# A fused MoE, MoE, attention and FFN kernel: set-up reordered, the second half's routing rescheduled, attention maxima held in 16-bit halves

## The chip, the cores and the metric

The kernel runs on one core of one Trainium2 chip as a single program. The metric is the device time of one execution in microseconds. The engines are TensorE (PE, whose weight loads PEld overlap its matmuls), VectorE (DVE), ScalarE (ACT), GpSimd (POOL) and the queues that start DMA transfers (SP, and those of ACT, DVE and POOL).

## The reference, cut to what matters

x is 32 x 128 x 128, so 4096 tokens of width 128; ctx has the same shape. Four residual layers follow one another, each on a layer norm of x:

```python
x = x + moe_a(layernorm(x), ctx)    # 8 experts 128->512->128, relu; router on ctx, top 2, softmax of the two
x = x + moe_b(layernorm(x))         # 16 experts 128->128->128, silu(x W1+b1)*(x W3+b3); sigmoid scores,
                                    # best 2 of 4 groups, top 4 of 16, weights * 2.5 / their sum
x = x + attention(layernorm(x), ctx, ctx)  # 16 heads of 8, masked to earlier keys, softmax(q k / sqrt(8)) v
x = x + 0.5 * ffn(layernorm(x))     # integer weights scaled, 128->512->128 with silu

def attention(q, k, v):             # qh, kh, vh: heads of 8 columns
    mask = triu(ones(S, S), k=0); mask[0, 0] = False
    scores = where(mask, -inf, qh @ kh.T * scale)
    return softmax(scores) @ vh @ Wo.T + bo
```

The softmax needs the maximum of each row of scores, which is subtracted before the exponential.

## The kernel before

Tokens lie on partitions in tiles of 128; four tiles make a block of 512 (NT = 4), and there are 8 blocks (NB), in two halves of 4 (BH). The tensor X holds the running x for all blocks. fp32 products are built of a rounded high and a low half (`..h`, `..l`), so a weight is first copied by `split_high` (ACT) and `split_low` (DVE, POOL).

**Set-up.** The context's logits choose two experts for each token. Each expert's first weight is "folded" (one row is subtracted from the others): TensorE's `fold(k)`, L1809 to L1813, then on ACT a copy out of PSUM (L1499) and `split_high(k)` (L1471). TensorE's `prefix` (L1789 to L1794) counts tokens per expert and tile into cb_ps, which DVE's `tile_bases` (L836) reads; `inverse` turns slots into token numbers, which DVE casts to idx_sa (L899, `inverted`). ACT's `table_a` writes the normalised tokens of the first half to memory (a_tokens: L1485, L1492). POOL's `gather_slots` (L639) then gathers tokens by expert.

**Stage A** has 39 steps for each half, **stage B** 35 (SB) for each half. A step is one tile of 128 x 4 tokens of one expert (A) or of a group of four experts (B): TensorE transposes the gathered rows when a tile group begins (L1836), multiplies up and down, ACT applies the function, DVE forms products and the low halves (L1241 and L1244, L1252). The rows of results go to memory and are gathered back per token by POOL (`gather_a`, L647; `gather_b`, L669), and DVE adds them to X (`combine_a`, L1013 to L1021).

**The routing of the next stage** is done in the background: `background(h, T)` is called on DVE (L1137), ACT (L1545) and TensorE (L1885) at the end of step T of a half, and does what the tables of L273 to L279 put there. Each table has an entry per half: h = 0 (the first four blocks) runs in stage A's second half, h = 1 in stage B's first. CMB is `combine_a`, STT the statistics, APP the normalised rows, FWD the transposes, LOG the logits, SGM the sigmoid, GRP and MSK the choice of groups, PRE the counts, TOP the best four, POS the slots' bases, WTS the weights, HOT, EID and INV the inversion, SLT the cast of the slots to idx_sb, which POOL waits for before the second half's gathers. Nothing schedules at run time: each engine's instructions stand in program order, and semaphores join them. POOL's queue order is written out by hand (`gather_slots`, `gather_a`, `gather_b` and powers).

**Stage C** is the attention: 32 steps `tau`, each a block and one of four groups of four heads. TensorE computes the scores twice, by rows (`scores`, L2070 and L2071) for the maxima, and transposed (`scores_T`, L2082) for the exponentials; POOL masks the exponentials (L761, `mask_keys`); L2094 multiplies by the values. DVE takes the negated maxima (L1302, `max_of`) into negmax, and `split_max` writes them as two halves (a bf16 high part and the rest) into two columns of nmpad, a part of the tile brows. TensorE transposes nmpad (L2121) into tr_ps, and DVE adds the result to the queries (L1319), so that the next product subtracts the maximum. **Stage D** is the FFN.

## Time and profile before

| | |
|---|---|
| median of 3 runs | 1053.17 us (1051.47 to 1054.09) |
| profiled execution | 1050.84 us |
| its span | 1049.0 us |
| PE, PEld busy | 811.3 (77%), 621.0 (59%) |
| DVE, ACT, POOL busy | 636.2 (61%), 500.6 (48%), 395.2 (38%) |
| mean granted clock of TensorE | 0.876 |

By stretch, from the windows of the trace (us; busy us):

| stretch | us | PE | DVE | ACT | POOL | clock |
|---|---|---|---|---|---|---|
| set-up, 0 to 44.6 | 44.60 | 26.10 | 31.66 | 21.04 | 20.24 | 0.78 |
| stage A, to 370 | 325.40 | 238.54 | 160.49 | 132.35 | 106.67 | 0.85 |
| stage B, to 734 | 364.00 | 262.21 | 195.18 | 168.97 | 132.00 | 0.83 |
| stage C, to 982 | 248.00 | 224.87 | 198.28 | 127.51 | 134.02 | 0.98 |
| stage D, to 1049 | 67.00 | 59.57 | 50.56 | 50.77 | 2.29 | 0.93 |

An engine's busy time against the length of its stretch says how near that stage is to the engine's limit; the chain of waits says which engine's work or signal came last at each moment. "Another core or an unknown queue" in it is a semaphore event whose sender the profile does not name. "Issue" is time in which an engine waited for nothing that the profile shows. A row "x4" is four instructions one after another, whose time runs from the first start to the last end; matmuls overlap, so the time that a group of them really takes is read from the start of the group to the start of the next row.

### The profile page before, as it was taken

The page shows a single profiled execution, that of the slowest core. Times are in us where ns is not written, and L with a number is a line of the kernel's source. Part 1 is how long each engine was busy: PE and PEld are TensorE (multiplying, and loading weights), DVE is VectorE, ACT ScalarE, POOL GpSimd, SP SyncE. Part 2 cuts the span into 40 slices and gives each one's busy share as a digit, 9 for nine tenths or more (in the row PEclk, how much of TensorE's full clock was granted, in tenths as well). Part 3 has the DMA queues.
Part 4 walks back from the last instruction along what each step waited for, and adds up shares of the span by engine and source line. Part 5 has one row for each costly group of instructions (what it writes and reads, how often), then busy time and mean ns, then how long its engine had stood idle before and what let it go on. Part 6 is the DMA issues. An engine that isn't in the chain of part 4 may idle for free.

```text
span 1049.0 us, 17575 instructions
## 1 busy us (share of the span) xinstructions
PE 811.3 (77%) x5374; PEld 621.0 (59%) x5374; DVE 636.2 (61%) x1897; ACT 500.6 (48%) x984; POOL 395.2 (38%) x462
## 2 busy tenths in 40 slices
PE   6577187885789843769877566799789999989898
PEld 4475176764678733657666455688455555555575
DVE  5766053443555812557695344586778888887596
ACT  4443043442465422347644234476255555546586
POOL 5435733005510073443104545410466644446200
PEclk9589678898898965978988868799899999999899
DMA  8482246454311221171021131110344544543011
GB/s 286 132 269 92 87 116 196 164 200 145 103 49 39 71 67 27 42 282 41 23 66 44 53 102 42 57 29 22 105 129 133 139 119 118 165 114 107 5 31 50
DMA packets 96368, 106.54 MB, mean 102 GB/s; under 512 B 12604, under 2 KB 70348, under 8 KB 94999
## 3 DMA queue, kind: packets, MB, share of 16 engines
q1 hardware_dynamic: 76856, 78.04, 23.8%
q0 software_dynamic: 8608, 18.22, 6.8%
q10 hardware_dynamic: 10816, 9.16, 2.8%
q8 instruction: 48, 0.79, 0.3%
q14 instruction: 40, 0.33, 0.1%
HBM read 69.19 MB, written 36.18 MB: 100 GB/s over the span
## 4 chain that ended last, share of the span: by engine, by line
PE 50%; another core or an unknown queue 13%; issue 12%; DVE 11%; ACT 7%; POOL 3%; ACTq 1%; DMA 1%; SPq 1%; DVEq 0%; POOLq 0%
PE y_ps L1872 4%; PE y_ps L2094 3%; PE y_ps L1999 3%; PE hid_ps L1984 3%; PE hid_ps L1860 2%; PE hid_ps L2070 2%; PE hid_ps L2071 2%; PE hid_ps L2082 2%; PE hid_ps L1968 2%; PE tr_ps L2149 2%; PE hid_ps L1850 2%; PE tr_ps L2121 1%; PE hid_ps L1852 1%; PE hid_ps L1969 1%
## 5 line engine op out<-in xcount | busy, mean ns | idle before, releaser
L639 POOL DMA_INDIRECT xr<-b_tokens,idx_sb x70 | 67.0, 957 | 152.6 <-DVE idx_sb L899 105.7
L1121 DVE TENSOR_TENSOR hl<-hid_ps,hh 128x512 fp32r<-128x512 f32 x78 | 53.8, 690 | 110.7 <-ACT hh L1530 73.6
L1872 PE MATMUL y_ps<-region,hh 128*128 x312 | 91.8, 371 | 27.9 <-DVE hl L1121 16.6
L647 POOL DMA_INDIRECT yg<-a_rows,idx_a x64 | 60.9, 952 | 91.8 <-DMA a_rows<-yo 63.3
L1302 DVE TENSOR_REDUCE negmax<-hid_ps 128x4 f32<-128x512 f32 x128 | 85.8, 684 | 8.9 <-PE hid_ps L2071 7.9
L1872 PEld LDWEIGHTS y_ps<-region,hh 128*128 128x128 f32 x312 | 64.8, 208 | 37.0 <-issue 36.6
L1984 PE MATMUL hid_ps<-ident,zb 128*128 128x128 f32 x280 | 49.5, 306 | 45.9 <-DVE hl L1252 24.2
L1860 PE MATMUL hid_ps<-ident,zb 128*128 128x128 f32 x312 | 53.7, 301 | 38.8 <-issue 24.3
L1524 ACT ACTIVATE zb<-hid_ps 128x512 f32<-128x512 f32 x78 | 46.6, 597 | 77.1 <-PE hid_ps L1852 38.8
L1999 PE MATMUL y_ps<-region,hh 128*128 x280 | 82.1, 369 | 0.1
L1241 DVE TENSOR_TENSOR zb<-hid_ps,sg 128x256 f32<-128x256 f32 x70 | 29.7, 424 | 85.5 <-ACT sg L1626 51.3
L2071 PE MATMUL hid_ps<-region 128*128 128x512 f32 x128 | 76.5, 599 | 0.0
L669 POOL DMA_INDIRECT yg<-b_rows,idx_b x64 | 61.3, 958 | 38.6 <-issue 36.7
L1984 PEld LDWEIGHTS hid_ps<-ident,zb 128*128 128x128 f32 x280 | 38.2, 158 | 63.4 <-issue 39.0
L1860 PEld LDWEIGHTS hid_ps<-ident,zb 128*128 128x128 f32 x312 | 43.6, 157 | 53.6 <-issue 27.7
L1620 ACT ACTIVATE sg<-hid_ps 128x512 f32<-128x512 f32 x70 | 41.7, 596 | 68.4 <-PE hid_ps L1970 34.6
L1874 PE MATMUL y_ps<-region,hl 128*128 x312 | 73.1, 234 | 0.0
L1252 DVE TENSOR_TENSOR hl<-hid_ps,hh 128x512 fp32r<-128x512 f32 x70 | 47.9, 684 | 31.4 <-issue 19.8
L1633 ACT ACTIVATE hh<-hid_ps 128x512 fp32r<-128x512 f32 x70 | 41.0, 585 | 54.4 <-remote 28.4
L1874 PEld LDWEIGHTS y_ps<-region,hl 128*128 128x128 f32 x312 | 65.9, 211 | 0.0
L2001 PE MATMUL y_ps<-region,hl 128*128 x280 | 65.5, 234 | 0.2 <-issue 0.2
L761 POOL TENSOR_SCALAR_AFFINE_SELECT sg<-sg 128x512 f32<-128x512 f32 x64 | 40.6, 634 | 58.9 <-ACT sg L1682 58.9
(354 smaller groups left out, 2365.1 us busy)
## 6 DMA issues: line engine op xcount, KB each, us to landing
region<-k_strips SPq DMA_DIRECT2D x128, 64.0 KB
region<-k_strips SPq DMA_DIRECT2D x32, 256.0 KB
region<-hl SPq DMA_DIRECT2D x128, 64.0 KB
k_strips<-k_halves SPq DMA_DIRECT2D x24, 256.0 KB
region<-nought SPq DMA_DIRECT2D x6, 1024.0 KB
a_rows<-yo SPq DMA_DIRECT2D x20, 256.0 KB
b_rows<-yo SPq DMA_DIRECT2D x18, 256.0 KB
staged<-a_w_in SPq DMA_DIRECT2D x16, 256.0 KB, 5.8
```

Of the source, the lines that this page charges most:

```text
L639: g.indirect_dma_start(xr[:, q % 3, j * RB:j * RB + w], None, src, bass.IndirectOffsetOnAxis(ap=rows.bitcast(U32), axis=0)).then_inc(x_got ...
L647: g.indirect_dma_start(yg[:, b % 2, k, j * P:(j + 1) * P], None, ys[h], bass.IndirectOffsetOnAxis(ap=idx[:, h, k, t:t + 1].bitcast(U32), a ...
L669: g.indirect_dma_start(yg[:, b % 2, k, j * P:(j + 1) * P], None, ys_b[h], bass.IndirectOffsetOnAxis(ap=idx_b[:, h, k, t:t + 1].bitcast(U32 ...
L1121: v.tensor_tensor(hl[:, n % 2, :], hid_ps[2 + n % 2][:], hh[:, n % 2, :].bitcast(F32), ALU.subtract).then_inc(a_hl, 1)
L1302: v.tensor_reduce(negmax[:, s % 2, b, :], hid_ps[b % 2][:].rearrange("p (i k) -> p i k", i=HG), AX, ALU.max, negate=True).then_inc(c_max, 1)
L1860: ins = t.transpose(hid_ps[2 + n % 2][:, cs], zb[:, n % 2, cs], ident[:])
L1872: t.matmul(y[:, c0:c0 + 2 * P], hh[:, n % 2, cs], w2a[:, bass.ds(e * (2 * FA) + c * 2 * P, 2 * P)], start=c == 0, stop=False)
L1874: t.matmul(y[:, c0:c0 + P], hl[:, n % 2, cs], w2a[:, bass.ds(e * (2 * FA) + c * 2 * P, P)], start=False, stop=False)
L1984: ins = t.transpose(hid_ps[3][:, es], zb[:, m % 2, es], ident[:])
L1999: t.matmul(y[:, c0:c0 + 2 * P], hh[:, m % 2, es], w2b[:, bass.ds(g * (2 * BT) + e * 2 * P, 2 * P)], start=e == 0, stop=False)
L2001: ins = t.matmul(y[:, c0:c0 + P], hl[:, m % 2, es], w2b[:, bass.ds(g * (2 * BT) + e * 2 * P, P)], start=False, stop=e == EG - 1)
L2071: t.matmul(hid_ps[b % 2][:], qp[s % QPS][:, b * P:(b + 1) * P], kdiag[s % KDS][:, b, :], start=False, stop=True).then_inc(c_s1, 1)
```

## The change

Three parts.

1. **Tables for the second half (h = 1).** The four combines move from steps 3, 7, 11, 15 to 5, 10, 14, 18, with the statistics in the same step instead of the next; what follows them moves too, down to the cast of the slots, from step 31 to 32. HOT (28) and INV (30) stay.
2. **Set-up.** ACT unfolds weights 0 to 3, writes the four tables of tokens, and then unfolds 4 to 7; before it unfolded all eight first. TensorE's counts (`prefix`) stand between fold 3 and fold 4. ACT's wait for in_last comes after the first copy.
3. **Maxima.** nmpad is a bf16 tile instead of fp32. The tile nm16 and one of the two casts are gone, the subtraction reads the high half from nmpad itself, and TensorE's four fp32 transposes are four bf16 matmuls against a bf16 identity.

```diff
--- before.py
+++ after.py
@@ -161,7 +161,7 @@
         att = wideflat[:, 0:2 * BT].rearrange("p (s v) -> p s v", s=2)
         cpad = brows[:].bitcast(F32)
         osb = cpad[:, 0:BT]
-        nmpad = cpad[:, BT:2 * BT].rearrange("p (b h r) -> p b h r", b=NT, h=HG)
+        nmpad = brows[:, 2 * BT:3 * BT].rearrange("p (b h r) -> p b h r", b=NT, h=HG)
         accT = yo
         scales = yg[:, 0]
         d_mv = rt[:, 0:NB * NT * 2].rearrange("p (b t k) -> p b t k", b=NB, t=NT)
@@ -173,7 +173,6 @@
         v_out, wkv = flat(sg[:])[:, 0:VW], flat(sg[:])[:, VW:VW + 2 * P]
         b2h = sb("b2h", [P, 1])
         negmax = sb("negmax", [P, 2, NT, HG])
-        nm16 = sb("nm16", [P, 2, NT, HG], BF16)
         rden = sb("rden", [P, NT, HG])
         b2b = sb("b2b", [EB, P])
         combT = xnt[0:EB, :]
@@ -270,13 +269,13 @@
             T = n % S
             return T % 2 == 1 or T == S - 1
 
-        CMB = ((6, 9, 13, 18), (3, 7, 11, 15))
...
+        CMB = ((6, 9, 13, 18), (5, 10, 14, 18))
...
         SGM, GRP, MSK, PRE, TOP, POS, WTS, HOT, EID, INV, SLT = (
-            (23, 20), (24, 22), (25, 23), (25, 24), (28, 23), (26, 25), (30, 27), (31, 28), (34, 31), (33, 30), (35, 31))
+            (23, 23), (24, 24), (25, 25), (25, 25), (28, 26), (26, 26), (30, 28), (31, 28), (34, 32), (33, 30), (35, 32))
         CH, PAIRS = 4, 8
         ESC = 2
         KVB = (4, 5, 0, 1, 2, 3, 6, 7)
@@ -1307,9 +1306,8 @@
                 eng.wait_ge(c_max, NT * s + NT)
                 if s:
                     eng.wait_ge(c_nmt, s)
-                link(v.tensor_copy(nm16[:, s % 2], negmax[:, s % 2]))
-                v.tensor_copy(nmpad[:, :, :, 3 * HD], nm16[:, s % 2])
-                v.tensor_tensor(nmpad[:, :, :, 3 * HD + 1], negmax[:, s % 2], nm16[:, s % 2], ALU.subtract).then_inc(c_nm, 1)
+                link(v.tensor_copy(nmpad[:, :, :, 3 * HD], negmax[:, s % 2]))
+                v.tensor_tensor(nmpad[:, :, :, 3 * HD + 1], negmax[:, s % 2], nmpad[:, :, :, 3 * HD], ALU.subtract).then_inc(c_nm, 1)
 
             def shift_queries(s):
 
@@ -1493,19 +1491,25 @@
 
             for b in range(BH):
                 load_x(b)
-            eng.wait_ge(in_last, 16)
-            for k in range(EA):
+            def unfold(k):
                 eng.wait_ge(fold_mm, k + 1)
                 a.activation(fold_buf(k)[0:P - 1, :], hid_ps[k % 4][0:P - 1, :], ACT.Copy).then_inc(folded, 1)
                 eng.wait_ge(folded, k + 1)
+                if k == 0:
+                    eng.wait_ge(in_last, 16)
                 split_high(k)
+
+            for k in range(EA // 2):
+                unfold(k)
             eng.wait_ge(nb_ready, 1)
             table_a(0)
             table_a(1)
             eng.wait_ge(nb_ready, 2)
             table_a(2)
             table_a(3)
-            for k in range(8, NRAW_A):
+            for k in range(EA // 2, EA):
+                unfold(k)
+            for k in range(EA, NRAW_A):
                 split_high(k)
 
             def x_high(q):
@@ -1813,10 +1817,12 @@
                 t.matmul(hid_ps[k % 4][:], less_last, raw_buf(k), start=True, stop=True).then_inc(fold_mm, 1)
 
             logits(0)
-            for k in range(EA):
+            for k in range(EA // 2):
                 fold(k)
             eng.wait_ge(chosen, 1)
             prefix(EA, 0)
+            for k in range(EA // 2, EA):
+                fold(k)
             for c in range(CH):
                 inverse(0, c, GA * NT, flat((xr[:], raw[:])[c // 2]).bitcast(F16), flat(yo[:]).bitcast(F16))
             logits(1)
@@ -2118,7 +2124,8 @@
                         eng.wait_ge(c_norm, tau - 1)
                     last_block_use(tau - 1)
                     for b in range(NT):
-                        ins = t.transpose(tr_ps[:, b * P:(b + 1) * P], nmpad[:, b].rearrange("p h r -> p (h r)"), ident[:])
+                        ins = t.matmul(tr_ps[:, b * P:(b + 1) * P], nmpad[:, b].rearrange("p h r -> p (h r)"), ident16[:],
+                                       start=True, stop=True)
                     ins.then_inc(c_nmt, 1)
                 if 0 <= tau + 3 < STEPS:
                     scores(tau + 3, 1)
```

**Order on ACT in set-up.** staged holds the folded weights (one of four PSUM buffers hid_ps is copied into it), region1 the rounded ones, wide the normalised tokens. Before:

```order
L1471 ACTIVATE region1<-staged 128x512 [waits in_raw0,folded]
L1499 ACTIVATE staged<-hid_ps0 127x512 [waits fold_mm]
L1471 ACTIVATE region1<-staged 128x512 [waits in_raw1,folded]
L1499 ACTIVATE staged<-hid_ps1 127x512 [waits fold_mm]
L1471 ACTIVATE region1<-staged 128x512 [waits in_raw1,folded]
L1499 ACTIVATE staged<-hid_ps2 127x512 [waits fold_mm]
L1471 ACTIVATE region1<-staged 128x512 [waits in_raw1,folded]
L1499 ACTIVATE staged<-hid_ps3 127x512 [waits fold_mm]
L1471 ACTIVATE region1<-staged 128x512 [waits in_raw1,folded]
L1485 ACTIVATE wide<-X,nbias,rstds 128x127 [waits nb_ready]
L1485 ACTIVATE wide<-X,nbias,rstds 128x127 x3
L1492 DMA a_tokens<-wide 128x4x128 [waits row_a]
```

Now:

```order
L1469 ACTIVATE region1<-staged 128x512 [waits in_raw0,folded]
L1483 ACTIVATE wide<-X,nbias,rstds 128x127 [waits nb_ready]
L1483 ACTIVATE wide<-X,nbias,rstds 128x127 x3
L1490 DMA a_tokens<-wide 128x4x128 [waits row_a]
L1483 ACTIVATE wide<-X,nbias,rstds 128x127 x4
L1490 DMA a_tokens<-wide 128x4x128 [waits row_a]
L1483 ACTIVATE wide<-X,nbias,rstds 128x127 [waits nb_ready]
L1483 ACTIVATE wide<-X,nbias,rstds 128x127 x3
L1490 DMA a_tokens<-wide 128x4x128 [waits row_a]
L1483 ACTIVATE wide<-X,nbias,rstds 128x127 x4
L1490 DMA a_tokens<-wide 128x4x128 [waits row_a]
L1496 ACTIVATE staged<-hid_ps0 127x512 [waits fold_mm]
```

Before, all eight folds (hid_ps0 to hid_ps3 twice) stand ahead of the first row of wide; now four do, and the fifth fold's copy out of hid_ps0 comes behind the fourth store to a_tokens.

**Order on DVE at the end of stage B's first half.** small, raw and gsel are small tiles of the routing, idx_b and idx_sb the row numbers that POOL gathers by; zb and hl belong to the step's products, yo to the rows of results, xTl to the transposed tokens of the second half. Before:

```order
L882 TENSOR_TENSOR raw<-raw 128x32 [waits dve]
L883 TENSOR_TENSOR idx_b<-raw 128x32 [waits dve]
L899 CAST idx_sb<-cb_ps 128x36 [waits inv_mm]
L1241 TENSOR_TENSOR zb<-hid_ps2,sg 128x256 [waits b_hT,b_up,b_sw]
L1244 SCALAR_TENSOR_TENSOR zb<-hid_ps2,w4,sg 128x128 x2
L1252 TENSOR_TENSOR hl<-hid_ps3,hh 128x512 [waits b_down,b_hh]
L1129 TENSOR_TENSOR yo<-yo,y_ps1 128x256 [waits b_yc]
L1241 TENSOR_TENSOR zb<-hid_ps1,sg 128x256 [waits b_hT,b_up,b_sw]
L1244 SCALAR_TENSOR_TENSOR zb<-hid_ps1,w4,sg 128x128 x2
L1252 TENSOR_TENSOR hl<-hid_ps3,hh 128x512 [waits b_down,b_hh]
L1105 TENSOR_TENSOR xTl<-tr_ps,xTh 128x512 [waits b_up,s_xh]
```

Now:

```order
L851 CAST eid_b<-small 128x36 [waits dve]
L853 TENSOR_TENSOR gsel<-small,firsts 128x144
L878 TENSOR_SCALAR raw<-raw 128x32
L879 TENSOR_SCALAR raw<-raw 128x32
L880 TENSOR_SCALAR raw<-raw 128x32
L881 TENSOR_TENSOR raw<-raw 128x32 [waits dve]
L882 TENSOR_TENSOR idx_b<-raw 128x32 [waits dve]
L898 CAST idx_sb<-cb_ps 128x36 [waits inv_mm]
L1240 TENSOR_TENSOR zb<-hid_ps1,sg 128x256 [waits b_hT,b_up,b_sw]
L1243 SCALAR_TENSOR_TENSOR zb<-hid_ps1,w4,sg 128x128 x2
L1251 TENSOR_TENSOR hl<-hid_ps3,hh 128x512 [waits b_down,b_hh]
L1104 TENSOR_TENSOR xTl<-tr_ps,xTh 128x512 [waits b_up,s_xh]
```

Before, the cast of idx_sb (with the small operations on raw ahead of it, of which two are shown) stood ahead of two steps' work on zb and hl and of the sum into yo; now one step's zb and hl are left behind it, and then comes the second half's xTl.

**Order on DVE in stage C.** hid_ps are the scores, brows is the tile in which nmpad lies, region1 the queries. Before:

```order
L1302 TENSOR_REDUCE negmax<-hid_ps1 128x4 [waits c_s1]
L1310 CAST nm16<-negmax 128x16 [waits c_nmt,c_max]
L1311 CAST brows<-nm16 128x16 [waits dve]
L1312 TENSOR_TENSOR brows<-negmax,nm16 128x16
L1399 TENSOR_TENSOR region1<-y_ps1,region1 128x512 [waits c_qh]
L1302 TENSOR_REDUCE negmax<-hid_ps0 128x4 [waits c_nm,c_s1]
L1319 TENSOR_TENSOR hl<-region2,tr_ps 128x512 [waits q_ld0,c_nmt]
```

Now:

```order
L1301 TENSOR_REDUCE negmax<-hid_ps1 128x4 [waits c_s1]
L1309 CAST brows<-negmax 128x16 [waits c_nmt,c_max]
L1310 TENSOR_TENSOR brows<-negmax,brows 128x16 [waits dve]
L1397 TENSOR_TENSOR region1<-y_ps1,region1 128x512 [waits c_qh]
L1301 TENSOR_REDUCE negmax<-hid_ps0 128x4 [waits c_nm,c_s1]
L1317 TENSOR_TENSOR hl<-region2,tr_ps 128x512 [waits q_ld0,c_nmt]
```

Two casts and a subtraction became one cast and a subtraction, and the subtraction waits for the cast (dve) where the second cast waited for the first.

## Rows read from the trace of the kernel before

**Rows 1.** The page's part 4: the chain by engine, shares of the span.
```profile
PE 50%; another core or an unknown queue 13%; issue 12%; DVE 11%; ACT 7%; POOL 3%; ACTq 1%; DMA 1%; SPq 1%; DVEq 0%; POOLq 0%
```

**Rows 2.** Stage C by windows: us, busy us per engine (instructions), clock, DMA share, GB/s.
```profile
734.00:982.00 248.00, 224.87 (x1865) 130.10 (x1864) 198.28 (x541) 127.51 (x223) 134.02 (x174) 0.98 0.44 120
```

**Rows 3.** Timeline of ScalarE in set-up: start us, us, instruction, [idle before <-releaser].
```profile
24.84 0.63 ACT L1471 ACTIVATE region<-staged 128x512 fp32r<-128x512 f32 x1
...
25.38 1.63 ACT L1485 ACTIVATE wide<-X,nbias,rstds 128x127 f32<-128x127 f32 x4
...
33.32 0.37 ACTq L1492 DMA_DIRECT2D a_tokens<-wide  x1
```

**Rows 4.** Timeline of set-up on the other engines: same columns.
```profile
21.20 0.15 DVE L970 SCALAR_TENSOR_TENSOR nbias<-mvs,rstds 128x8 f32<-128x8 f32 x1
...
23.63 0.42 DVE L836 SCALAR_TENSOR_TENSOR zb<-cb_ps,firsts 128x256 f32<-128x256 f32 x1 [2.28 <-PE cb_ps L1794]
...
35.61 0.20 DVE L899 CAST idx_sa<-cb_ps 128x40 int32<-128x40 f32 x1
...
37.55 1.15 POOL L639 DMA_INDIRECT xr<-a_tokens,idx_sa  x1 [13.12 <-DMA a_tokens<-wide]
...
44.62 1.11 PE L1836 MATMUL tr_ps<-ident,xr 128*128 128x128 f32 x4 [2.24 <-DMA xr<-a_tokens,idx_sa]
```

**Rows 5.** Timeline of VectorE: a combine of the second half.
```profile
420.64 2.32 DVE L1021 SCALAR_TENSOR_TENSOR X<-yg,gates,X 128x128 f32<-128x128 f32 x8
```

**Rows 6.** The chain of waits in stage B's first half: start us, us, what.
```profile
378.80 10.23 another core or an unknown queue
...
436.63 8.54 another core or an unknown queue
```

**Rows 7.** GpSimd alone by windows: us, busy us (instructions), clock, DMA share, GB/s.
```profile
364.30:404.40 40.10, 30.51 (x32) 0.66 0.24 67
...
557.50:572.40 14.90, 11.41 (x12) 0.77 0.27 72
572.40:580.20 7.80, 0.00 (x0) 1.00 0.13 43
```

**Rows 8.** Timeline round the end of stage B's first half.
```profile
547.65 1.09 PE L1984 MATMUL hid_ps<-ident,zb 128*128 128x128 f32 x4 [2.31 <-DVE hl L1252]
...
555.62 0.60 PE L1984 MATMUL hid_ps<-ident,zb 128*128 128x128 f32 x4
...
557.17 0.19 DVE L899 CAST idx_sb<-cb_ps 128x36 int32<-128x36 f32 x1
...
558.95 0.63 PE L1984 MATMUL hid_ps<-ident,zb 128*128 128x128 f32 x4 [0.42 <-DVE hl L1252]
...
563.98 0.66 PE L1836 MATMUL tr_ps<-ident,xr 128*128 128x128 f32 x4 [3.54 <-DMA xr<-b_tokens,idx_sb]
```

**Rows 9.** Timeline of TensorE: bf16 counts of set-up, and stage C.
```profile
22.49 0.22 PE L1789 MATMUL cb_ps<-m,before 128*128 128x128 bf16 x1
22.54 0.65 PE L1791 MATMUL cb_ps<-m,ones 128*128 128x120 bf16 x15
...
846.82 0.66 PE L2121 MATMUL tr_ps<-ident,brows 128*128 128x128 f32 x4
847.32 0.38 PE L2070 MATMUL hid_ps<-maskq,ident 128*128 128x512 bf16 x1
...
853.95 0.63 PE L2121 MATMUL tr_ps<-ident,brows 128*128 128x128 f32 x4 [0.47 <-DVE region L1375]
```

**Rows 10.** Timeline of stage C; last row: L1311's group, min/median/max ns.
```profile
846.02 0.63 POOL L761 TENSOR_SCALAR_AFFINE_SELECT sg<-sg 128x512 f32<-128x512 f32 x1 [0.80 <-ACT sg L1682]
846.11 0.58 DVE L1311 CAST brows<-nm 128x16 f32<-128x16 bf16 x1
...
846.59 0.17 DVE L1312 TENSOR_TENSOR brows<-negmax,nm 128x16 f32<-128x16 f32 x1
...
L1311 DVE CAST brows<-nm x32: 182/588/626, 737.6 to 961.6; 128x16 f32<-128x16 bf16 x32
```

More of the change, by code:

```diff
@@ L271, in ends_pair @@
             return T % 2 == 1 or T == S - 1
-        CMB = ((6, 9, 13, 18), (3, 7, 11, 15))
-        STT = ((7, 10, 14, 19), (4, 8, 12, 16))
-        APP = ((11, 13, 17, 20), (7, 11, 15, 17))
-        FWD = ((13, 15, 19, 22), (9, 13, 17, 19))
-        LOG = ((14, 16, 20, 23), (10, 14, 18, 20))
+        CMB = ((6, 9, 13, 18), (5, 10, 14, 18))
+        STT = ((7, 10, 14, 19), (5, 10, 14, 18))
+        APP = ((11, 13, 17, 20), (9, 14, 18, 20))
+        FWD = ((13, 15, 19, 22), (11, 16, 20, 22))
+        LOG = ((14, 16, 20, 23), (12, 17, 21, 23))
         SGM, GRP, MSK, PRE, TOP, POS, WTS, HOT, EID, INV, SLT = (
-            (23, 20), (24, 22), (25, 23), (25, 24), (28, 23), (26, 25), (30, 27), (31, 28), (34, 31), (33, 30), (35, 31))
+            (23, 23), (24, 24), (25, 25), (25, 25), (28, 26), (26, 26), (30, 28), (31, 28), (34, 32), (33, 30), (35, 32))
         CH, PAIRS = 4, 8
```

## The prediction

> **What bounds the kernel now.** I read the chain of waits first. Half of it is TensorE at work; the next share, 13% or some 136 us, is "another core or an unknown queue", and DVE has 11% [rows 1]. One core runs, so that share is a signal that the profile can't assign. By stretch (the table ahead) stage C is the nearest to TensorE's limit: 224.87 us of 248.00 busy [rows 2]. Set-up and stage B wait for other things. The three parts of the change fall into these three kinds of place, so each is priced where it lies. All sums are against the profiled execution of 1050.84 us (span 1049.0), which lies 2.33 below the median of 1053.17; I add that at the end.
>
> **Set-up: -4.0 us.** ACT copies the last folded weight at 24.84 and only at 25.38 begins the normalised rows that go to memory as a_tokens; the fourth store is issued at 33.32 [rows 3]. POOL waits for these rows (13.12 us of idle time) and starts its first gather at 37.55, TensorE its first transpose of tokens at 44.62 [rows 4]. In the new order the rows come after four folds instead of eight. Four pairs of ACT (a copy out of the fold, then the rounding copy of 0.63 at 24.84, which with its turn-over takes 0.54 until 25.38; both kinds are of one size, so some 1.2 a pair) would be 4.9 us earlier; but the rows also need nbias, written by DVE at 21.20 and ready at 21.35 [rows 4]. So they start at 21.4, which is 4.0 before 25.38, and the last store goes out at 29.3. The gather needs slots as well: idx_sa is written at 35.61, behind tile counts that DVE takes from cb_ps at 23.63 after 2.28 us of waiting for TensorE [rows 4]. The count matmuls now stand ahead of folds 4 to 7, which gives back most of these 2.28 us: idx_sa at about 33.4, before the rows land (37.55-4.0 = 33.5). So 37.55 becomes 33.5, and 44.62 becomes 40.6. What is late next: the low halves of the weights on DVE, whose order doesn't change, and the second four folds, which now come after the stores on ACT: four pairs from about 29.7, so 34.6, then the same roundings as before, in time for an up-projection that can't start before the transposes at 40.6. Bounds: -2 (idx_sa becomes the last, the 2.2 alone is won) to -5 (the full four pairs and no new wait).
>
> **The second half's combines and statistics: 0.** This is the same DVE work (the combine takes 2.32 us [rows 5]), so only waiting could be won. At 420.64 a combine of the second half starts without idle time before it [rows 5], and POOL had issued the 32 gathers of that stretch by 404.4 [rows 7]. A combine moved later therefore takes no wait away. One wait of the page is the reverse: POOL's gathers wait for a combine to free a buffer, once, and the combine that now comes later frees it later. Bounds -2 to +2, by the order of DVE's work within a step.
>
> **The unassigned waits: 0.** The chain has one of 10.23 us at 378.80 and one of 8.54 at 436.63 [rows 6]. Both fall where POOL issues gathers one behind another: 32 in 364.3 to 404.4, of which it is busy 30.51 us [rows 7]. Where POOL issues only pairs of gathers (stage C) the chain has no such piece. The number of gathers in each burst and what they wait for are the same after the change, so I leave these 136 us as they are. They are where a small shift can cost most, and one rival uses them.
>
> **Routing packed closer: +2.3.** The tables for the second half now put groups, masks, counts, best choices and weights into steps 23 to 28 instead of 20 to 27, with the count matmuls of TensorE one step behind the groups instead of two. The work is the same. Spread over fewer steps, more of them hold more than a step can hide. A late DVE stops TensorE at once: at 547.65 its transposes had waited 2.31 us for DVE's low half, behind the routing's work of that step [rows 8]. I take one more wait of this size, +2.3. Bounds 0 (the work that is squeezed finds idle time) and +4.6 (two).
>
> **Slots one step later: +3.3.** idx_sb is cast on DVE at 557.17, and POOL, which has nothing else to do there, starts the gathers of the second half at once; TensorE has finished the first half and stands for 3.54 us at 563.98 until rows arrive [rows 8]. That is a wait on the path, and the change puts the cast (and the eleven small operations ahead of it) one step later. A step here is 555.62 to 558.95 between two groups of transposes, 3.33 us [rows 8]. So the gather and 563.98 move back by 3.3. Bounds: +1 (the step that the block leaves runs quicker, and TensorE with it) and +5 (a step with a wait for DVE in it, 3.33 and some of 2.31).
>
> **Maxima in 16 bits, TensorE: -5.6.** Per head group TensorE transposes the padded maxima in four fp32 matmuls: begun at 846.82, the next matmul begins at 847.32, so 0.50 us [rows 9]. Four bf16 matmuls of 128 columns: the nearest row is the count matmul with 128 columns, begun at 22.49 with the next at 22.54, which is 0.05 each and 0.21 for four [rows 9]. The difference is 0.28, times 32 steps is 9.0. Not all of it counts. Where DVE is last it is lost: TensorE waited 0.47 at 853.95 for DVE, which was adding up queries, not for the maxima [rows 9]. One step in four has such a chain, through POOL's power and DVE, and the steps with gathers have more; I take 12 of 32 as lost. 20 by 0.28 is 5.6. Bounds 0 and 9.0.
>
> **Maxima in 16 bits, DVE: -0.9.** Before there are three operations: a rounding cast, the widening cast (0.58 at 846.11) and the subtraction (0.17 at 846.59) [rows 10]. The middle one is the dear one, and its time is not its own: over 32 occurrences it takes 182 ns at least, 588 in the median [rows 10]. It starts 0.09 us after POOL's mask, which begins at 846.02 and lasts 0.63 [rows 10], and it ends with it. In the new order this cast is gone, but the subtraction, now with a bf16 tile of memory as its second input, starts in its place, some 0.08 us into the same mask. Either it is held up like the cast it replaces, and no more than one short operation of 0.17 is saved, or it runs free and about 0.6 us are saved. I take the nearest row, the operation that starts at the same moment on the same tile: held up, some 0.1 saved in each of about eight steps where DVE is last, which makes 0.8, and 0.1 ahead of the first step. With the page's other rows I can't show it: the old subtraction started at 846.59, when the mask was all but over. The Trainium skill, "SBUF — State Buffer", section "Who interferes with whom", says that a vector instruction with two inputs in SBUF contends with a GpSimd instruction that reads SBUF, and that a cast in a two-port mode locks the shared ports for as long as it runs. The trace agrees for the cast (588 against 182 ns); for two inputs no row shows it. By that rule the saving is the small one; without it, the first rival's. Bounds -6 and 0.
>
> **Sum.** -4.0 + 0 + 0 + 2.3 + 3.3 - 5.6 - 0.9 = -4.9, so 1045.9 for an execution like the profiled one, and 1045.9 + 2.3 = 1048.2 against the median. With the parts' bounds leaning the same way only in part, its own range is 1044.5 to 1051.5.
>
> **The rivals.**
> (a) The subtraction runs free beside the mask. Then each step's DVE work falls by 0.57 more. About eight steps where DVE is last (0.47 at 853.95 is one of them [rows 9]) give 0.57 each: 4.6 us, so 1043.6. For it: the old subtraction took 0.17 every time. Against it: it never lay beside a mask. Chance 0.20.
> (b) Given back. The earlier start of stage A meets an unassigned wait whose end is set by POOL's queue and by memory, and stage C saves TensorE time that other chains fill. Then set-up gives 1 and stage C 3, routing costs 4: the profiled 1050.84 stays, 1053.2 against the median. For it: the 13% [rows 1] and the many places in stage C where POOL or ACT is last. Against it: nothing between 44.6 and 364 waits for a fixed time. Chance 0.15.
> (c) Slower, by the pause in POOL's queue. The first 12 gathers of the second half take 557.5 to 572.4, then POOL stands still for 7.8 us until the last rows of the first half are in memory, and then issues 16 more [rows 7]. The first burst moves back by 3.3, the release of the second does not move with it. If the pause shrinks below what keeps the two apart, 28 gathers form one burst. The chain's pieces are 10.23 us beside 32 gathers and 8.54 beside 12 [rows 6, 7], so a second such piece of 8 to 10 appears on the path: 1048.2 + 9.4 = 1057.6. It decides from a pause of some 4 us downwards; by my sum it stays 4.5, at the edge. For it: the nearness. Against it: POOL's release may move back too, since TensorE's stores do. Chance 0.14.
> That the change does not do what it says is part of the forecast: the moved combines had no gathers to wait for.
>
> **How the numbers follow.** Forecast 0.50, (a) 0.20, (b) 0.15, (c) 0.14, 0.01 unnamed. A measurement of this kernel can tell 0.3%, 3.2 us, from no change: faster is below 1050.0, slower above 1056.3. Of the forecast's own range 0.44 lies below 1050.0 and 0.06 above; (a) is faster throughout, (b) is no change in 0.13 and slower in 0.01, (c) is slower in 0.12 and no change in 0.02. Faster 0.64, same 0.22, slower 0.14. The range 1041 to 1055.5 takes in (a), the forecast and (b), and leaves (c) out.
>
> **What would show it.** In the profile after: the first gather at 33.5 and TensorE's first token transpose at 40.6 (right), or a gather that waits for idx_sa (bound of -2). The cast of idx_sb about 3.3 us later than the shift of the stage itself, and TensorE's wait for its first rows grown from 3.5 to 6.8. From the bf16 group to the next matmul 0.21. The new subtraction beside the mask near 0.59 us (forecast) or near 0.18 (a). Stage C shorter than 248.00 by 6 to 7. The pause between the 12 and the 16 gathers above 4 us; if it is gone and the chain has a new piece of 8 us or more there, it is (c). The forecast is wrong if the combines of the second half turn out to have stood waiting, if the idle of TensorE between steps 23 and 28 falls instead of rising, or if stage B's unassigned waits change by more than 5 us.

## The result, and the profile after

The changed kernel takes 1061.02 us (1059.44 to 1065.82, 8 runs) against 1053.93 for the kernel before in the same series (1051.47 to 1058.38, 8 runs): ratio 1.0079, interval 1.0055 to 1.0103. It is slower by 8.3 us by this ratio. 1048.2 was forecast, with a range to 1055.5. Its profiled execution took 1060.29 us, span 1057.8. (Lines shift in the changed kernel: L1252 is L1251, L1626 is L1630, L1836 is L1842, L1984 is L1990.)

Set-up first, from the timelines of ACT, VectorE, GpSimd and TensorE after, one row each (start us, us, instruction, idle before it):

```profile
22.18 0.15 DVE L969 SCALAR_TENSOR_TENSOR nbias<-mvs,rstds 128x8 f32<-128x8 f32 x1
22.37 1.64 ACT L1483 ACTIVATE wide<-X,nbias,rstds 128x127 f32<-128x127 f32 x4 [1.72 <-DVE nbias L969]
...
30.32 0.37 ACTq L1490 DMA_DIRECT2D a_tokens<-wide  x1
...
34.23 0.20 DVE L898 CAST idx_sa<-cb_ps 128x40 int32<-128x40 f32 x1
...
34.73 1.32 POOL L638 DMA_INDIRECT xr<-a_tokens,idx_sa  x1 [10.47 <-DVE idx_sa L898]
...
42.14 1.12 PE L1842 MATMUL tr_ps<-ident,xr 128*128 128x128 f32 x4 [1.14 <-DMA xr<-a_tokens,idx_sa]
```

The rows of wide start 3.0 us earlier than in [rows 3] and not 4.0, since nbias comes 1.0 later than in [rows 4]. The gather starts at 34.73 instead of 37.55 and now waits for idx_sa, which won 1.4. TensorE is 2.5 ahead at 42.14. The slots' list has become the last to arrive.

Now the stretches. I cut stage B by its gates (`gate(m)`, the silu on ACT): gate 0, 20, 34, 36 and 69. Windows of the kernel before (us, then PE, PEld, DVE, ACT, POOL busy with their instructions, granted clock, DMA share, GB/s), the last one stages C and D from the first mask on:

```profile
375.36:498.13 122.77, 76.88 (x445) 64.72 (x445) 56.98 (x198) 52.15 (x119) 56.35 (x60) 0.78 0.27 91
498.13:557.88 59.75, 49.55 (x341) 42.71 (x341) 47.50 (x149) 33.43 (x72) 3.63 (x5) 0.90 0.14 40
557.88:574.92 17.04, 11.59 (x63) 9.67 (x61) 5.78 (x18) 4.65 (x10) 11.15 (x12) 0.80 0.25 67
574.92:727.14 152.22, 115.02 (x659) 98.13 (x657) 79.50 (x238) 72.62 (x164) 56.73 (x61) 0.85 0.18 51
755.77:1049.00 293.23, 268.21 (x2069) 165.28 (x2068) 233.85 (x644) 173.34 (x298) 126.96 (x166) 0.98 0.37 100
```

The same of the kernel after:

```profile
376.63:499.96 123.33, 77.37 (x444) 66.60 (x443) 54.42 (x183) 49.59 (x111) 51.99 (x55) 0.77 0.27 89
499.96:568.15 68.19, 50.91 (x344) 44.07 (x343) 49.44 (x154) 36.18 (x80) 7.78 (x8) 0.87 0.13 38
568.15:588.35 20.20, 11.38 (x54) 9.57 (x53) 6.88 (x28) 4.54 (x11) 11.42 (x12) 0.66 0.21 57
588.35:740.65 152.30, 113.54 (x667) 96.61 (x667) 79.25 (x238) 72.83 (x164) 56.11 (x61) 0.85 0.18 51
767.79:1057.80 290.01, 260.67 (x2069) 157.50 (x2068) 232.42 (x615) 173.04 (x298) 127.83 (x166) 0.99 0.37 102
```

Gate 0 is 1.3 us behind although stage A began 2.5 ahead. Gates 20 to 34 cost 8.4 more, of which TensorE's busy time has 1.4; gates 34 to 36, with the wait for the second half's first rows, 3.2 more; the next stretch nothing. From gate 69 to the first mask 1.5 are saved, and in stages C and D behind it 3.2. Part of what appears between gates 20 and 34 was only moved there: the fourth block's rows and transposes stood before gate 20.

What TensorE waits for between gates 20 and 34, first before, then after (engine, group, what it waited for: us in total, times, longest):

```profile
PE hid_ps L1984 <- DVE hl L1252: 7.6, 5, 2.6
PE hid_ps L1968 <- ACT sg L1620: 1.5, 1, 1.5
PE hid_ps L1984 <- issue: 1.1, 1, 1.1
```

```profile
PE hid_ps L1990 <- DVE hl L1251: 13.3, 6, 4.5
PE cb_ps L1793 <- DVE m L1045: 3.1, 1, 3.1
PE hid_ps L1974 <- ACT sg L1624: 0.8, 1, 0.8
```

5.7 us more behind VectorE's low halves and a new wait of 3.1 for the groups' mask, which VectorE now writes in the step in which TensorE counts (before, one step ahead). ACT after, in the same place:

```profile
521.12 0.22 ACT L1566 ACTIVATE rt<-cb_ps 128x64 f32<-128x64 f32 x1 [1.04 <-PE cb_ps L1904]
521.37 1.28 ACT L1569 ACT_TABLE_LOAD   x1
522.66 0.42 ACT L1569 ACTIVATE rt<-rt 128x256 f32<-128x256 f32 x1
523.10 1.28 ACT L1624 ACT_TABLE_LOAD   x1
524.39 0.60 ACT L1624 ACTIVATE sg<-hid_ps 128x512 f32<-128x512 f32 x1
```

ACT waits for the fourth block's logits, loads a table for the sigmoid and another to go back, and only then does the gate's silu. VectorE stands for it:

```profile
525.75 0.42 DVE L1240 TENSOR_TENSOR zb<-hid_ps,sg 128x256 f32<-128x256 f32 x1 [4.58 <-ACT sg L1630]
```

The cast of the slots and what hangs on it:

```profile
570.66 0.19 DVE L898 CAST idx_sb<-cb_ps 128x36 int32<-128x36 f32 x1
...
577.43 1.11 PE L1842 MATMUL tr_ps<-ident,xr 128*128 128x128 f32 x4 [7.32 <-DMA xr<-b_tokens,idx_sb]
```

TensorE's wait has grown from 3.54 [rows 8] to 7.32. In stage C the padded maxima go through TensorE in 859.56 - 859.32 = 0.24 us instead of 0.50 [rows 9]:

```profile
859.32 0.40 PE L2127 MATMUL tr_ps<-ident,brows 128*128 128x128 bf16 x4
...
859.56 0.38 PE L2076 MATMUL hid_ps<-maskq,ident 128*128 128x512 bf16 x1
```

and the subtraction on VectorE is held up beside the mask as the cast was in [rows 10] (ns, min/median/max):

```profile
L1310 DVE TENSOR_TENSOR brows<-negmax,brows x32: 228/605/645, 751.1 to 971.8; 128x16 bf16<-128x16 f32 x32
```

### The profile page after: what moved, and what is told of

Read it like the earlier page. It is cut to its first block, busy times and chain, and to the rows that moved or that the text cites. A ratio compares the mean times of both kernels' runs of the same rounds, so it can differ in the third digit from the quotient of the medians.

```text
span 1057.8 us, 17541 instructions
## 1 busy us (share of the span) xinstructions
PE 803.6 (76%) x5374; PEld 615.7 (58%) x5374; DVE 635.1 (60%) x1865; ACT 501.3 (47%) x984; POOL 396.0 (37%) x462
## 4 chain that ended last, share of the span: by engine, by line
PE 45%; issue 16%; another core or an unknown queue 14%; DVE 13%; ACT 5%; POOL 4%; DMA 2%; ACTq 1%; SPq 0%; DVEq 0%; POOLq 0%
PE y_ps L1878 4%; PE hid_ps L1866 3%; PE y_ps L2005 2%; PE y_ps L2100 2%; PE hid_ps L1990 2%; PE hid_ps L1856 2%; PE tr_ps L2156 2%; PE hid_ps L1974 2%; PE hid_ps L2076 2%; PE hid_ps L2077 2%; PE hid_ps L2088 2%; PE hid_ps L1858 1%; PE hid_ps L1857 1%; PE y_ps L1880 1%
## 5 line engine op out<-in xcount | busy, mean ns | idle before, releaser
L638 POOL DMA_INDIRECT xr<-b_tokens,idx_sb x70 | 67.1, 959 | 156.2 <-DVE idx_sb L898 108.7
L1878 PE MATMUL y_ps<-region,hh 128*128 x312 | 94.0, 377 | 26.0 <-issue 14.4
L1528 ACT ACTIVATE zb<-hid_ps 128x512 f32<-128x512 f32 x78 | 46.5, 597 | 78.6 <-PE hid_ps L1858 39.7
L2005 PE MATMUL y_ps<-region,hh 128*128 x280 | 82.7, 372 | 0.1
L1990 PE MATMUL hid_ps<-ident,zb 128*128 128x128 f32 x280 | 48.2, 301 | 43.9 <-DVE hl L1251 28.9
L668 POOL DMA_INDIRECT yg<-b_rows,idx_b x64 | 61.4, 959 | 38.6 <-issue 36.2
L1990 PEld LDWEIGHTS hid_ps<-ident,zb 128*128 128x128 f32 x280 | 37.7, 156 | 60.1 <-issue 30.4
L1251 DVE TENSOR_TENSOR hl<-hid_ps,hh 128x512 fp32r<-128x512 f32 x70 | 47.8, 682 | 25.3 <-issue 18.9
```

What stands on the lines that cost most here:

```text
L638: g.indirect_dma_start(xr[:, q % 3, j * RB:j * RB + w], None, src, bass.IndirectOffsetOnAxis(ap=rows.bitcast(U32), axis=0)).then_inc(x_got ...
L668: g.indirect_dma_start(yg[:, b % 2, k, j * P:(j + 1) * P], None, ys_b[h], bass.IndirectOffsetOnAxis(ap=idx_b[:, h, k, t:t + 1].bitcast(U32 ...
L1878: t.matmul(y[:, c0:c0 + 2 * P], hh[:, n % 2, cs], w2a[:, bass.ds(e * (2 * FA) + c * 2 * P, 2 * P)], start=c == 0, stop=False)
L1990: ins = t.transpose(hid_ps[3][:, es], zb[:, m % 2, es], ident[:])
L2005: t.matmul(y[:, c0:c0 + 2 * P], hh[:, m % 2, es], w2b[:, bass.ds(g * (2 * BT) + e * 2 * P, 2 * P)], start=e == 0, stop=False)
```

## The experiments

Each job ran its kernels and the kernel before on one chip. The chips differ, and are named by their numbers in the record: on chips 0 and 10 the kernel before takes 1054 and 1063 us, on chips 6 and 11 897 and 896. (The series of the result has 1054 as well.) Each ratio is one within a job, so it stands, but a wait can weigh differently on another chip; the last section comes back to it.

**The three parts alone.** Tables of the second half only:

```diff
-        CMB = ((6, 9, 13, 18), (3, 7, 11, 15))
+        CMB = ((6, 9, 13, 18), (5, 10, 14, 18))
...
-            (23, 20), (24, 22), (25, 23), (25, 24), (28, 23), (26, 25), (30, 27), (31, 28), (34, 31), (33, 30), (35, 31))
+            (23, 23), (24, 24), (25, 25), (25, 25), (28, 26), (26, 26), (30, 28), (31, 28), (34, 32), (33, 30), (35, 32))
```

> The kernel before with the new step tables of the second half alone; set-up and maxima as before. Theory D (dense routing on VectorE): the changed kernel's trace is level until step 22 of stage B's first half and 10 us behind at its step 34, so the tables alone cost 10 to 14 us: ratio 1.010 to 1.013. Rival P (phase): the loss comes from stage A's start having moved against GpSimd's bursts; then the tables alone cost what the forecast said, about 5.6 us, or nothing. Rival C (two bursts of gathers run together) would show 8 to 10 us at step 36 and little before it.

Measured 1.0086 (1.0052 to 1.0120), 9.1 us. Maxima only (the diff's hunks on nmpad, nm16, `split_max` and the bf16 matmuls):

> The kernel before with the 16-bit maxima alone. The forecast's term: -6.5 us. In the changed kernel's trace stage C gives back 3.7 us only (12.5 us behind at its start, 9 at the end), so theory D expects -3.5 to -4.5 us, ratio 0.996 to 0.9965. If the cast had locked less than forecast it would be near -9.

Measured 0.9970 (0.9939 to 1.0000), -3.2 us. Set-up only (the hunks on `unfold` and `fold`):

> The kernel before with the reordered set-up alone. The forecast's term: -4.0 us. The changed kernel is 2.5 us ahead at stage A's first step and 0 to 1 us behind from its step 18 on, so theory D expects 0 to +1.5 us (ratio 1.000 to 1.0015), with the gain gone at steps 16 to 18. Rival P expects several us slower by the start of stage B.

Measured 0.9973 (0.9941 to 1.0005), -2.8 us; this interval takes in 1, so by time the gain is not shown for this part alone. The trace is 3.0 us ahead at stage A's first step and still 4.5 ahead at gate 0: the lead was not lost here, against what I expected from the changed kernel's trace. Changed kernel with the tables of before:

> The changed kernel with the step tables of before: set-up and maxima changed. Theory D: the sum of the two, -2 to -4 us against before, ratio 0.996 to 0.998. Rival P: about as slow as the changed kernel, 1.005 or more.

Measured 0.9955 (0.9926 to 0.9984). So the tables are the loss, and the other two parts gain 4.7 us together. From 0.9955 to 1.0079 (two jobs) the tables cost 1.24%, 13 us.

**The tables taken apart.** These ran on chip 6. Combines, statistics, rows and logits early, the rest late:

```diff
-            (23, 20), (24, 22), (25, 23), (25, 24), (28, 23), (26, 25), (30, 27), (31, 28), (34, 31), (33, 30), (35, 31))
+            (23, 23), (24, 24), (25, 25), (25, 25), (28, 26), (26, 26), (30, 28), (31, 28), (34, 32), (33, 30), (35, 32))
```

> The kernel before, with the second half's combines, statistics, rows and logits where they were, but the tables from SGM to SLT as in the changed kernel (23 24 25 25 26 26 28 28 32 30 32). Theory D (the cost lies in steps 23 to 32: routing packed behind step 23, then slots one step later): nearly the whole loss of the tables alone, 7 to 11 us slower than before, ratio 1.007 to 1.010. Rival M (the moved combines, statistics and transposes cost): at most 4 us, the slots' 3.3 and little else.

Measured 1.0091 (1.0062 to 1.0120). The front moved and the rest of before:

```diff
-        CMB = ((6, 9, 13, 18), (3, 7, 11, 15))
+        CMB = ((6, 9, 13, 18), (5, 9, 12, 15))
...
-        LOG = ((14, 16, 20, 23), (10, 14, 18, 20))
+        LOG = ((14, 16, 20, 23), (11, 15, 18, 20))
```

> The kernel before with combines and statistics moved and put in one step, (5 9 12 15) for both, rows (8 12 15 17), transposes (10 14 17 19), logits (11 15 18 20), and everything from SGM on as before. Theory D: 0 +-2 us, ratio 0.998 to 1.002, since the combines waited for nothing where they were. Rival M: 4 to 8 us slower.

Measured 1.0017 (0.9995 to 1.0039). The new tables with EID and SLT at 31:

> The kernel before with the changed tables, only EID and SLT back at step 31 (routing still packed in 23 to 28). Theory D, second term: the slots' step is worth its 3.3 us, so 3 to 4 us better than the tables alone, and still 5 to 7 us slower than before: ratio 1.005 to 1.007. If the packing costs nothing: 1.000 to 1.002.

Measured 1.0086 (1.0058 to 1.0114): more than expected, so the rest of the tables costs more than 7 us on this chip. One step earlier than before (HOT 27, INV 29, EID and SLT 30):

> The kernel before with HOT 27, INV 29, EID and SLT 30 instead of 28, 30, 31, 31 in the second half. TensorE stood 3.54 us for the second half's first rows, so one step earlier should win up to 3.3 us at the second half's first step if the slot's term is right: ratio 0.997 to 0.998. Against it, the operations of steps 27 to 30 are packed closer; if packing is dear, 1.000 or more.

Measured 0.9978 (0.9956 to 1.0001). Next, the new tables again, in another job on chip 6:

> The new tables alone, once more, so that all pieces of them are timed on one chip with it. About 9 us slower than before: ratio 1.008 to 1.011, whatever the theory.

Measured 1.0173 (1.0148 to 1.0198), 15.5 us: nearly twice as much as on chip 0 (9.1), not what I had written. Against the same tables with EID and SLT at 31 (1.0086, the job before) that is 7.8 us for one step of the slots, where the traces below show 2.8 in the stretch of the slots: times from different jobs are uncertain by some microseconds even on one chip. Packed (SGM 23 to WTS 28), EID and SLT 31, early front:

> The kernel before with SGM to INV of the changed kernel, while the combines stay early and EID and SLT stay at 31. Theory D (packing): most of the loss, 5 to 7 us (1.005 to 1.008), of which 3.1 us is TensorE's wait for the mask, which DVE now writes in the step in which TensorE counts. Rival M2 (the late last combine leaves no step between logits, sigmoid and groups): packing alone costs 3 us (1.003), and the rest of the tables' loss beyond the slots' 3.3 needs the moved combines.

Measured 1.0068 (1.0040 to 1.0096). Only EID and SLT 32:

> The kernel before with EID and SLT of the second half at 32 instead of 31 and nothing else. In the traces the pause of TensorE ahead of the second half's first rows grows by 3.3 us for each step by which the cast is late (7.0, 10.1 and 13.6 us from one gate to the next for casts at 30, 31 and 32), so +3.3 us: ratio 1.0025 to 1.004. If the pause is filled by other late work: 1.000 to 1.001.

Measured 1.0056 (1.0034 to 1.0079). The packed tables with MSK 24:

> Like the packed tables with EID and SLT at 31, but the groups' mask at step 24, one ahead of TensorE's counts at 25, instead of in the same step. If TensorE's wait of 3.1 us for the mask is on the path, 2 to 3 us less than e10_packed_31; if VectorE's amount of work is what costs, the same as e10_packed_31 or slower, since step 24 then holds groups and mask together.

Measured 1.0049 (1.0028 to 1.0069), not told apart from 1.0068. TensorE still waits 3.1 us for the mask, presumably because VectorE now does groups and mask in one step; the edit didn't remove the wait, so what it costs stays open.

By then the pieces did not add up to the whole. The front moved as above, with the fourth block's combine left at 15, and the late rest:

> The kernel before with combines and statistics at (5 9 12 15), rows (8 12 15 17), transposes (10 14 17 19), logits (11 15 18 20), and the changed kernel's tables from SGM on (slots at 32): the changed tables with the last block's combine at 15 instead of 18. Rival M2 (the late last block leaves no step between logits, sigmoid and groups): as the late tail alone plus the moved front, 1.009 to 1.011 on a chip where the tables cost 1.017, and in the trace steps 22 to 27 level with the kernel of moved combines alone. Theory F (moving the combines costs by itself): 1.015 or more.

Measured 1.0107 (1.0063 to 1.0151), on chip 10: too wide to decide. The trace does: gates 20 to 34 take 59.0 us, as before. Then, on chip 11, only the fourth block late (with the late rest), and the new tables beside it:

```diff
-        CMB = ((6, 9, 13, 18), (3, 7, 11, 15))
+        CMB = ((6, 9, 13, 18), (3, 7, 11, 18))
...
-        LOG = ((14, 16, 20, 23), (10, 14, 18, 20))
+        LOG = ((14, 16, 20, 23), (10, 14, 18, 23))
```

> The kernel before with only the fourth block moved as in the changed kernel (combine and statistics 18, rows 20, transposes 22, logits 23) and the tables from SGM on as in the changed kernel; the first three blocks as before. Rival M2 (the last block's late logits, with sigmoid in the same step and groups in the next, cost the part at steps 22 to 27): the whole loss of the tables, and in the trace 6 to 9 us lost between steps 21 and 27. Theory F (the first blocks' moves cost): like the late tail alone, with 1 us lost between 21 and 27.

> The new tables alone on the same chip as e17_last_late, for comparison: 1.008 to 1.009 where the chip shows unassigned waits, 1.017 where it shows none. Rival M2: within 0.003 of e17_last_late. Theory F: at least 0.005 above it.

Measured 1.0128 (1.0103 to 1.0153) and 1.0153 (1.0132 to 1.0173). They come within 0.003. The late tail alone had 1.0091 (1.0062 to 1.0120), in another job; its interval touches the first of these, so by time alone the fourth block is not told from the tail. The traces have to tell.

The stretches of these traces (us from gate to gate, one profiled execution each, on chip 6 where nothing else is said):

| tables | 0 to 20 | 20 to 34 | 34 to 36 |
|---|---|---|---|
| front moved, rest of before | 78.5 | 57.0 | 13.4 |
| slots 30 | 78.4 | 57.6 | 10.7 |
| slots 32 | 77.7 | 57.0 | 17.3 |
| packed, slots 31 | 78.3 | 59.3 | 14.8 |
| packed, mask 24, slots 31 | 79.2 | 61.4 | 13.3 |
| late tail | 78.5 | 59.2 | 18.2 |
| fourth block late too (chip 11) | 76.3 | 66.0 | 17.6 |
| all new, slots 31 | 78.6 | 65.6 | 14.8 |
| all new (second run, and third on chip 11) | 78.4, 76.2 | 67.1, 66.0 | 17.6, 16.9 |
| before (chip 0) | 122.8 | 59.7 | 17.0 |
| front of 15, late tail (chip 10) | 133.4 | 59.0 | 20.3 |

Between gates 20 and 34 the four profiles with the late fourth block on chips 6 and 11 lie at 65.6 to 67.1 and the six without it at 57.0 to 61.4. On chips 0 and 10 the two kernels with the new tables need 67.7 and 68.2, six with the old tables (the kernel before, set-up only, both maxima kernels, statistics in the combine's step, changed kernel with old tables) 59.1 to 62.5. One outlier with old tables and slots 30 needs 64.6 (the gains together, below). So the 8.4 us between the two profiles of the first section are one value out of a range of 5 to 9.

Windows from gate 20 to 34 of slots 32, of packed with slots 31, and of the fourth block late:

```profile
401.37:458.39 57.02, 48.12 (x340) 41.62 (x339) 46.59 (x140) 33.86 (x72) 3.79 (x4) 0.91 0.15 42
```

```profile
401.66:460.96 59.30, 48.23 (x340) 41.44 (x339) 47.71 (x151) 33.30 (x73) 4.06 (x5) 0.91 0.14 41
```

```profile
400.40:466.40 66.00, 50.80 (x341) 42.86 (x340) 49.62 (x155) 34.98 (x75) 7.78 (x8) 0.87 0.14 39
```

TensorE's waits in the last one:

```profile
PE hid_ps L1984 <- DVE hl L1252: 10.0, 6, 3.3
PE cb_ps L1789 <- DVE m L1046: 3.1, 1, 3.1
PE hid_ps L1968 <- ACT sg L1620: 1.8, 2, 1.0
```

The packed kernel has 7.5 us in four waits for hl and the same 3.1; the one with slots 32 has 7.6 and no wait for the mask. The late fourth block adds 2.5 us of waits for VectorE, and 2.6 us of TensorE's busy time, at a granted clock of 0.87 against 0.91; whether the lower clock is a cause of the loss or comes of it is not shown.

Gate by gate the two kernels (packed, and fourth block late) can be laid side by side; they differ by 0.3 us up to gate 15. Two rows of ScalarE in the second:

```profile
409.40 0.88 ACT L1485 ACTIVATE wide<-X,nbias,rstds 128x127 f32<-128x127 f32 x2 [1.56 <-DVE nbias L970]
...
418.73 0.23 ACT L1562 ACTIVATE rt<-cb_ps 128x64 f32<-128x64 f32 x1 [1.03 <-PE cb_ps L1898]
```

The fourth block's rows (first row) lengthen gate 21 to 22 from 4.1 to 7.0 us, but they shorten 18 to 19, where they stood, from 5.2 to 2.5: moved, not added. Gate 19 to 20, where combine and statistics now stand, takes 0.9 more. Gate 24 to 25, with the sigmoid, takes 6.1 instead of 4.9, and 1.03 of that is ScalarE's wait for the logits (second row), which it doesn't have in the packed kernel. Gates 27 to 33 take 2.3 more, of which 1.5 lie in one gate (32 to 33), where kernels with the old tables vary just as much (2.7 to 4.9).

The slots' step is clean in the third column: on chip 6, each step by which the cast is late adds 2.7 to 3.9 us. With slots 30, then 32, TensorE's first rows of the second half:

```profile
461.11 0.65 PE L1836 MATMUL tr_ps<-ident,xr 128*128 128x128 f32 x4 [1.21 <-DMA xr<-b_tokens,idx_sb]
```

```profile
467.70 1.11 PE L1836 MATMUL tr_ps<-ident,xr 128*128 128x128 f32 x4 [7.36 <-DMA xr<-b_tokens,idx_sb]
```

**Maxima, TensorE's part alone** (nmpad in 16 bits and bf16 matmuls; VectorE keeps three operations):

> The kernel before with only TensorE's part of the maxima: a 16-bit padded tile and bf16 matmuls, while VectorE keeps its two casts and the tile nm16. The forecast gave TensorE 5.6 of 6.5 us; the whole came to 3.2. If all of that is TensorE's: 0.996 to 0.997. If VectorE's short operation less carries it: 0.999 to 1.001.

Measured 0.9993 (0.9962 to 1.0024): the time can't tell. The trace can. Its window from the first mask to the end:

```profile
773.51:1063.60 290.09, 260.70 (x2069) 157.35 (x2068) 234.49 (x644) 173.17 (x298) 127.17 (x166) 0.99 0.37 102
```

290.1 against 293.2 before, as much as the four kernels with the whole change have (289.9 to 290.0). Four others on chips 0 and 10 that keep the fp32 maxima lie at 293.0 to 293.8. So the 3.1 us are TensorE's, and VectorE's part is worth nothing that these windows show.

**Statistics in the combine's step** (STT of the second half 3 7 11 15):

> The kernel before with the statistics of the second half in the same step as their combine (3 7 11 15), nothing else moved. The same work in a lump of 3.8 us instead of 2.3 and 1.5: 0 to +2 us (1.000 to 1.002) if a step hides the lump; 3 us or more (1.003) if each lump sticks out of its step.

Measured 1.0036 (1.0001 to 1.0071); gates 20 to 34 take 59.1. The lump seems to cost a little; the interval nearly reaches 1.

**The gains together, with slots 30:**

> The changed set-up and maxima with the tables of before, but HOT 27, INV 29, EID and SLT 30. Sum of the parts: set-up -2.5, maxima -3.2, slots -2 us: ratio 0.991 to 0.994. If gains on different stages are lost in waits between them: 0.996 to 0.999.

Measured 1.0002 (0.9978 to 1.0027): a miss. Stage A starts 3.0 us earlier and stages C and D take 289.9, but gates 20 to 34 take 64.6 and 34 to 36 take 20.2 here. In this profile unassigned waits are 15% of the chain, and single profiles differ: for stage A's first 18 steps the kernels in this job with the old set-up need 93.6 to 94.4 us, this one 93.1, and the kernel before 89.2 on chip 0. What took the gains back is open. They were seen by time on chip 0 (0.9955) and not on chip 10. So I have no version that is shown to beat the kernel before by more than the changed kernel with the old tables, 0.9955.

## Why the prediction was wrong

The sign was wrong: a gain of 0.5% was forecast, and the kernel lost 0.8%. By times the distance of 13.2 us (-4.9 forecast, +8.3 measured) splits in two: the tables cost 13 on top of the other parts where the terms gave 5.6, and set-up and maxima together gave 4.7 where they gave 10.5. The first of these turned the sign. By its steps:

- **Combines and statistics, 0: the step that failed.** True that no gather was waited for, and that was all the term looked at. Moving the fourth block from 15 to 18 moves all that stands behind it (rows at 20, transposes at 22, logits and sigmoid at 23), and the forecast had no term for that. From gate 0 to 34 the late fourth block costs 142.3 - 137.6 = 4.7 us, 2.0 saved up to gate 20 and 6.7 lost after it. With all four blocks moved it is 142.2, 144.2 and 145.5, so the first three cost -0.1 to 3.2 more in single profiles; the times, 1.0128 against 1.0153 and 1.0173, leave 2 to 4 us with touching intervals. That share is not settled. Of the mechanism one piece is in the rows: ScalarE's wait of 1.03 us for logits ahead of the sigmoid and its two table loads. In the changed kernel it is 1.04, and the silu behind them is 4.58 us late for VectorE; in the kernel before the same sigmoid followed its logits without a wait, and the groups came two steps behind it instead of one. It accounts for about 1.3 of the 4.7; the rest is spread over the steps, and no run isolates it.
- **Routing packed closer, +2.3: about right in size, not in kind.** From gate 0 to 34, 137.6 us against 134.7 to 136.0 with the old tail, so 1.6 to 2.9 (by time 3.6 to 8.6 us for the packed tables with slots 31). The one new wait of 2.3 was expected for VectorE's low half; what came is one of 3.1 for the mask. The forecast had counted the steps from groups to counts (two, now one) and not those from mask to counts (one, now none). That the sum of waits fits is partly luck.
- **Slots one step later, +3.3: right.** 34 to 36 grows by 2.7 to 3.9 us a step; after, TensorE's wait is 7.32, where 6.8 was forecast.
- **Set-up, -4.0: too large.** -2.8 by time, with an interval to nothing, and 2.5 to 3.0 at stage A's first step. Two causes, both in the rows: nbias came 1.0 later, and idx_sa gained 1.4 instead of 2.2 and was the last. The lower bound named that case.
- **Maxima, TensorE -5.6: too large.** The group shrank by 0.26 us (0.28 forecast), but only 3.1 of 32 x 0.26 = 8.3 us reached the end. 20 of 32 steps was too high; 12 is what the windows give. Stage C's TensorE is busy for 90% of it [rows 2], and still most of a shorter group did not reach the end; where it went was not followed up.
- **Maxima, VectorE -0.9: right in kind.** The subtraction with two inputs in memory lasts 605 ns beside the mask, as the Trainium skill, "SBUF — State Buffer", section "Who interferes with whom", says of two inputs; rival (a), the free subtraction, is refuted. When VectorE kept all three operations (TensorE's part alone), the middle copy took 608 and stages C and D were no longer, so the 0.9 was not seen.
- **Unassigned waits, 0: open.** Their share went from 13% to 14%, and gate 0 came 1.3 us late after a start 2.5 ahead, so in the profiles 5.3 of the 13.7 us by which the spans miss the forecast lie ahead of gate 0. The set-up alone kept its lead in one profile and the one without tables lost it (gate 0: -4.5 and +3.7 against before). With such a spread between single profiles this term can't be sized.
- **Rival (c), two bursts run together:** not the cause. GpSimd's pause between the 12 and the 16 gathers is 7.81 us in the changed kernel (from 585.90 to 593.71), as before, and not the 4.5 that was forecast: the release of the second burst moved back as well. Gates 36 to 69 take 152.3 us against 152.2.

On chip 0 the parts give -2.8 + 9.1 - 3.2 = 3.1, the whole 8.3. The intervals allow it (the tables up to 12.7 us), and so they don't say more.

## What to carry to other kernels

When work is moved later in a schedule written by steps, follow the chain behind it and count the steps between each producer and its consumer on another engine. Where none is left, the consumer waits, and what stands behind it on its engine is late too: here 3.1 us at the mask and 1.04 at the logits, with the silu behind them. Whether the moved instruction itself had to wait is only the first question. A list that the next phase's first transfer needs (the slots here) can cost its whole delay, if the phase already begins with a wait for it. And a gain of 0.3% that one chip shows can be missing on another: time the parts together again before relying on their sum.

## What the runs showed of the hardware

The same kernel takes 1054 us on chip 0 and 897 on chip 6, and nearly all of the difference sits in the stretches in which GpSimd issues gathers. With slots 32 (the kernel before but for one step) on chip 6, gates 0 to 20 and 36 to 69:

```profile
323.67:401.37 77.70, 69.77 (x447) 60.21 (x446) 56.26 (x198) 51.15 (x120) 56.41 (x60) 0.96 0.44 144
475.66:580.11 104.45, 101.70 (x679) 89.34 (x678) 78.21 (x238) 73.26 (x164) 57.87 (x62) 1.00 0.28 75
```

122.77 and 152.22 us on chip 0, for the same work, at granted clocks of 0.78 and 0.85 instead of 0.96 and 1.00. The ten profiles on chips 0 and 10 have 12% to 15% of their chain in the unknown queue; in none of the ten on chips 6 and 11 does the chain name it at all, as here for slots 32:

```profile
PE 55%; DVE 12%; issue 10%; POOL 8%; ACT 5%; DMA 4%; ACTq 3%; SPq 2%; DVEq 0%; POOLq 0%
```

Stages C and D, where no burst of gathers lies, take 290.2 to 293.3 us on chips 6 and 11 with the fp32 maxima, against 293.0 to 293.8 on chips 0 and 10; what sets the 3 us between kernels with the same code there I don't know, which is why the maxima were read on chips 0 and 10 alone. So the 13% in [rows 1] goes with the chip that a kernel happens to run on, together with bursts of gathers; what sends the late signals was not found. Pieces of a schedule are better compared where these are absent: the same tables cost 0.86% on chip 0 and 1.73 and 1.53% on chips 6 and 11.
